# Rings of eight and products four deep in a graph network's row expansions and sums

## What is computed

```python
edge_index = jnp.stack([src, dst])
...
x = _layernorm(x + _L1_gnn_ref(x, edge_index, L1_gnn_W, L1_gnn_b), axis=-1)
x = _layernorm(x + _L2_gnn_ref(x, L2_gnn_weight1, L2_gnn_weight2, src, dst), axis=-1)
x = _layernorm(x + _L3_gnn_ref(x, edge_index, edge_attr_16, batch0, L3_gnn_W, L3_gnn_a), axis=-1)
```

```python
h_src = feat_n[src]
copy_sum = jax.ops.segment_sum(h_src, dst, num_segments=N)
```

## Time and profile before

| | us |
|---|---|
| median of three runs | 16084.6 |
| lowest and highest | 16077.82, 16091.67 |
| the profiled execution | 16079.79 |
| its span | 16078.1 |

### The profile page before, as it was taken

One profiled execution on the slowest core, in us unless ns is written; L12 is line 12 of the kernel. 1 busy time (PEld: TensorE's weight loads), 2 busy tenths in 40 slices (PEclk: granted clock), 3 DMA queues, 4 the chain that ended last, 5 costly groups with the idle time before them and its releaser, 6 DMA issues. The chain is left out here.

```text
span 16078.1 us, 333902 instructions
## 1 busy us (share of the span) xinstructions
PE 10302.2 (64%) x72558; PEld 7980.5 (50%) x72559; DVE 10167.2 (63%) x36116; ACT 4495.2 (28%) x11901; POOL 9058.1 (56%) x10038
## 2 busy tenths in 40 slices
PE   6555555555537777767965656645566776667886
PEld 5333333333326666656853444422344664336886
DVE  9666666666643444437856777752365666887887
ACT  0111111111102333322113430025301223556886
POOL 0477777777745777767764445546400555554442
PEclk9777777777766777765556667755555665557998
DMA  9722222222242444453319997756653897885665
GB/s 369 303 80 79 81 81 79 79 83 79 79 94 58 80 80 80 80 79 71 68 28 279 324 309 223 224 163 218 191 176 89 279 278 257 270 267 204 212 212 160
DMA packets 2144346, 2589.93 MB, mean 161 GB/s; under 512 B 892242, under 2 KB 1761819, under 8 KB 2144195
## 3 DMA queue, kind: packets, MB, share of 16 engines
q1 hardware_dynamic: 1749158, 1741.66, 37.6%
q0 software_dynamic: 353792, 655.17, 13.1%
q10 hardware_dynamic: 41244, 191.56, 3.1%
HBM read 1738.44 MB, written 848.86 MB: 161 GB/s over the span
## 5 line engine op out<-in xcount | busy, mean ns | idle before, releaser
L566 POOL DMA_INDIRECT edges_by_dst<-rec,pos x1568 | 1541.2, 983 | 1029.1 <-DVE rec L501 555.5
L989 POOL DMA_INDIRECT sc_rows<-src_table,sc_idx x1664 | 1589.1, 955 | 607.9 <-issue 497.6
L566 POOL DMA_INDIRECT edges_by_cell<-rec,pos x1568 | 1545.5, 986 | 514.8 <-issue 497.4
L1756 PE MATMUL ex_rows<-table,ex_oh 128*128 x6528 | 1132.6, 339 | 884.8 <-DVE ex_stage L1732 335.7
L1844 PE MATMUL gs_part<-gs_rows,gs_oh 128*128 128x192 bf16 x6528 | 1024.4, 321 | 602.0 <-DVE gs_oh L1817 518.5
L1756 PEld LDWEIGHTS ex_rows<-table,ex_oh 128*128 128x128 bf16 x6528 | 724.9, 129 | 1292.3 <-issue 1252.6
L642 PE MATMUL xps<-ident,ea 128*128 128x128 f32 x784 | 216.4, 431 | 1740.9 <-DMA ea<-in_edge_attr_dram 1740.9
L1844 PEld LDWEIGHTS gs_part<-gs_rows,gs_oh 128*128 128x128 bf16 x6528 | 697.0, 131 | 929.3 <-issue 613.5
L2224 ACT ACTIVATE key_in_block<-at_rows,first_node 128x66 f32<-128x66 f32 x4352 | 1083.3, 336 | 266.2 <-PE at_part L2252 244.9
L2252 PE MATMUL at_part<-cell_edge_term,key_in_block 128*66 128x128 f32 x8704 | 1062.7, 286 | 115.3 <-issue 96.4
L530 DVE SCALAR_TENSOR_TENSOR junk<-rowb,keycol,earlier 128x128 f32<-128x128 f32 (+1 forms) x3136 | 1124.5, 415 | 1.8
(11 more groups left out here) (402 smaller groups left out, 27327.5 us busy)
## 6 DMA issues: line engine op xcount, KB each, us to landing
ex_keys<-src_key_rows SPq DMA_DIRECT2D x1632, 128.0 KB
gs_rows<-dst_rows_by_src SPq DMA_DIRECT2D x1088, 192.0 KB
rowb<-sort_key_rows SPq DMA_DIRECT2D x392, 512.0 KB, 5.2
ex_keys<-dst_key_rows SPq DMA_DIRECT2D x1088, 128.0 KB
dst_rows_by_src<-patY ACTq DMA_DIRECT2D x1, 104448.0 KB, 417.2
rows_by_src<-ex_stage SPq DMA_DIRECT2D x544, 192.0 KB
scored_dst_rows_by_src<-patZ ACTq DMA_DIRECT2D x1, 71808.0 KB, 637.9
scored_rows_by_src<-ex_stage SPq DMA_DIRECT2D x544, 132.0 KB
```

The lines of the kernel that those rows point to most:

```text
L566: nc.gpsimd.indirect_dma_start(out=out, out_offset=bass.IndirectOffsetOnAxis(ap=pos[:, u, k, j:j + 1], axis=0), in_=row, in_offset=None).t ...
L989: nc.gpsimd.indirect_dma_start(out=rows[:, u, j, :], out_offset=None, in_=tabS, in_offset=bass.IndirectOffsetOnAxis(ap=idx[:, u, j:j + 1], ...
L1756: m = nc.tensor.matmul(rows[k][u % 2][r // 2][:, r % 2, 0:W], oh[k][:, u % 2, r * P:(r + 1) * P], t3[:, bass.ds(held[k][u], 1), :].rearran ...
```

## The change

In `expand_rows`, a call with one list (ex2) gets rings of R = 8 key and staging slots and loops of eight steps, and one-hots and PSUM buffers that are four deep; with two lists (ex1) R = 4 and two deep stay. `sum_rows` gets four one-hot buffers and makes them three groups ahead (gs1 and gs2). `attention_rows` gets four one-hot and four PSUM buffers a list and makes the one-hots three ahead in place of two. `skewed` takes the number of steps of a turn as `ring`.

```diff
-def skewed(eng, n, stages, enter=None):
+def skewed(eng, n, stages, enter=None, ring=RING):
...
-        for u in range(RING):
-            step(i, u, 0 if isinstance(i, int) and i == 0 else None, RING if last else None)
+        for u in range(ring):
+            step(i, u, 0 if isinstance(i, int) and i == 0 else None, ring if last else None)
...
-    n = D.NG // RING
     lists = [q for q in ((0, K.krA, toA), (1, K.krB, toB)) if q[2] is not None]
+    R, deep = (RING, 2) if len(lists) == 2 else (2 * RING, 4)
+    n = D.NG // R
...
-        keys = {k: sb(f"keys{k}", [P, RING, SLOTS * P], BF16) for k, _, _ in lists}
-        oh = {k: sb(f"oh{k}", [P, 2, SLOTS * P], BF16) for k, _, _ in lists}
-        stage = {k: sb(f"stage{k}", [P, RING, SLOTS, W], BF16) for k, _, _ in lists}
-        rows = {k: [[ctx.enter_context(nc.psum_tensor(f"{name}_rows{k}{u}{h}", [P, 2, 256], F32)) for h in range(2)] for u in range(2)]
+        keys = {k: sb(f"keys{k}", [P, R, SLOTS * P], BF16) for k, _, _ in lists}
+        oh = {k: sb(f"oh{k}", [P, deep, SLOTS * P], BF16) for k, _, _ in lists}
+        stage = {k: sb(f"stage{k}", [P, R, SLOTS, W], BF16) for k, _, _ in lists}
+        rows = {k: [[ctx.enter_context(nc.psum_tensor(f"{name}_rows{k}{u}{h}", [P, 2, 256], F32)) for h in range(2)] for u in range(deep)]
...
-                        wait(sp, s_oh[k], g - RING + 1)
+                        wait(sp, s_oh[k], g - R + 1)
...
-                        wait(dve, s_mm[k], g - 1)
+                        wait(dve, s_mm[k], g - deep + 1)
...
-                skewed(dve, n, [(2, turn), (0, evict)])
+                skewed(dve, n, [(deep, turn), (0, evict)], ring=R)
...
-                        wait(pe, s_ev[k], g - 1)
+                        wait(pe, s_ev[k], g - deep + 1)
...
-        oh = {k: sb(f"oh{k}", [P, 2, P, SLOTS], BF16) for k, _, _ in lists}
+        oh = {k: sb(f"oh{k}", [P, RING, P, SLOTS], BF16) for k, _, _ in lists}
...
-                        wait(dve, s_mm[k], g - 1)
-                        nc.vector.tensor_tensor(oh[k][:, u % 2, :, :], K.iota4[:, :, :],
+                        wait(dve, s_mm[k], g - RING + 1)
+                        nc.vector.tensor_tensor(oh[k][:, u, :, :], K.iota4[:, :, :],
...
-                skewed(dve, n, [(1, onehots), (0, add)], blocks)
+                skewed(dve, n, [(3, onehots), (0, add)], blocks)
...
-        oh = [sb(f"oh{k}", [P, 2, SLOTS * P], BF16) for k in range(2)]
+        oh = [sb(f"oh{k}", [P, RING, SLOTS * P], BF16) for k in range(2)]
...
-        rows = [[ctx.enter_context(nc.psum_tensor(f"{name}_rows{k}{u}", [P, SLOTS, W], F32)) for u in range(2)] for k in range(2)]
+        rows = [[ctx.enter_context(nc.psum_tensor(f"{name}_rows{k}{u}", [P, SLOTS, W], F32)) for u in range(RING)] for k in range(2)]
...
-                skewed(dve, n, [(2, turn), (0, evict)])
+                skewed(dve, n, [(3, turn), (0, evict)])
...
-                        wait(pe, s_ev[k], g - 1)
+                        wait(pe, s_ev[k], g - RING + 1)
```

More of the change, by code:

```diff
@@ L697, in step @@
                 continue
-            run(i + q // RING, q % RING)
+            run(i + q // ring, q % ring)
     for s in range(-first, 0):
-        step(0, s, 0, n * RING)
+        step(0, s, 0, n * ring)
     def body(i, last):
@@ L704, in body @@
             enter(i)
-        for u in range(RING):
-            step(i, u, 0 if isinstance(i, int) and i == 0 else None, RING if last else None)
+        for u in range(ring):
+            step(i, u, 0 if isinstance(i, int) and i == 0 else None, ring if last else None)
     loop(eng, n, body)
-    for s in range(RING, RING + lastly):
-        step(n - 1, s, None, RING)
+    for s in range(ring, ring + lastly):
+        step(n - 1, s, None, ring)
 class Count:
@@ L1677, in expand_rows @@
         s_ev = {k: counts.get(f"expand_evicted{k}") for k, _, _ in lists}
-        s_out = {k: [counts.get(f"expand_stored{0 if back else k}{u}", back or k == 0) for u in range(RING)] for k, _, _ in lists}
+        s_out = {k: [counts.get(f"expand_stored{0 if back else k}{u}", back or k == 0) for u in range(R)] for k, _, _ in lists}
         with nc.Block() as block:
@@ L1694, in store @@
                                      stage[1][:, u, :, :].rearrange("p r c -> p (r c)")).then_inc(s_out[1][u].sem, 16)
-                skewed(sp, n, [(4, load), (-1, store)])
+                skewed(sp, n, [(4, load), (-1, store)], ring=R)
                 for k, _, _ in lists:
-                    for u in range(RING):
+                    for u in range(R):
                         wait(sp, s_out[k][u], n * 16)
@@ L1741, in evict @@
                         wait(act, s_out[1][u], i * 16)
-                        nc.scalar.copy(stage[1][:, u, 0:2, :], rows[1][u % 2][0][:, :, 0:W])
-                        nc.scalar.copy(stage[1][:, u, 2:4, :], rows[1][u % 2][1][:, :, 0:W]).then_inc(s_ev[1].sem, 1)
-                skewed(act, n, [(0, evict)])
+                        nc.scalar.copy(stage[1][:, u, 0:2, :], rows[1][u % deep][0][:, :, 0:W])
+                        nc.scalar.copy(stage[1][:, u, 2:4, :], rows[1][u % deep][1][:, :, 0:W]).then_inc(s_ev[1].sem, 1)
+                skewed(act, n, [(0, evict)], ring=R)
             @block.tensor
@@ L1761, in blocks @@
                     for k, _, _ in lists:
-                        held[k] = nc.values_load_multi_w_load_instructions(K.cblk[0:1, k, bass.ds(i * RING, RING)], engines=PE_ONLY,
+                        held[k] = nc.values_load_multi_w_load_instructions(K.cblk[0:1, k, bass.ds(i * R, R)], engines=PE_ONLY,
                                                                            min_val=0, max_val=D.blocks - 1, skip_runtime_bounds_check_because=CLAMPED)[1]
-                skewed(pe, n, [(0, products)], blocks)
+                skewed(pe, n, [(0, products)], blocks, ring=R)
         for k, _, _ in lists:
@@ L1843, in products @@
                         for r in range(SLOTS):
-                            m = nc.tensor.matmul(part[k][u][:, 0, :], oh[k][:, u % 2, :, r], rows[k][:, u, r, :],
+                            m = nc.tensor.matmul(part[k][u][:, 0, :], oh[k][:, u, :, r], rows[k][:, u, r, :],
                                                  start=r == 0, stop=r == SLOTS - 1)
@@ L1913, in turn @@
                         wait(dve, s_key[k][u], (i + 1) * 16)
[L1914 to L1915 removed]
+                        wait(dve, s_mm[k], g - RING + 1)
+                        nc.vector.tensor_scalar(oh[k][:, u, :], keys[k][:, u, :], K.iotac[:, :], None, ALU.is_equal).then_inc(s_oh[k].sem, 1)
                 def evict(i, u):
```

32 lines of the change are left out of this document (16 added, 16 removed).

## The result

The changed kernel takes 15,896.9 us (median of four runs, 15,888.2 to 15,899.6) against 16,081.2 us (16,077.2 to 16,091.7) for the kernel before: a ratio of 0.988, 95% interval 0.987 to 0.990. It is 184 us faster, where 272 us were forecast. Its profiled execution has a span of 15,897.9 us, that of before 16,078.1 us.

A forecast was written before the change was run, and what follows sets the result against it. It took staging slots to bound ex2, a DVE-PE ping-pong gs2, DVE's instructions gs1 and SyncE's stream ex3. 16079.8 - 125 (ex2) - 147 (gs2) = 15808, stated as 15810 us, range 15760 to 15905.

The forecast's parts named there:

- the ring of staging slots: ex2: four staging slots are the limit, 5.71 us for four groups; with eight slots the ring serves eight groups.
- POOL at 1.265 us a group: ex2: POOL's scatter issues are the next limit, 688 us plus a 6.25 us head, 694 in all; gain 125 us.
- rivals A: ex2: POOL's issue lengthens beside busy DVE and ACT, 1.44 us a group, 15903 us in all; chance 0.08.
- A2: ex2: full port lock, a one-hot before every issue, 1.61 us a group, 882 us, 15995 in all; chance 0.03.
- ACT's waits for the store: ex2: ACT's waits for a store to land would be gone after the change, as a sign of the forecast.
- The ping-pong: gs2: DVE and PE alternate with one one-hot ahead; removing two waits, 0.59 and 0.55 us, takes 4.48 to 3.34 a turn.
- the load ring: gs2: four slots for loaded rows are late next, 3.51 us a turn; 3.4 was taken, gain 147 us.
- the landing: gs2: time from a load's issue to its product, 2.51 us for the stage's first load, within 3.48 when steady.
- Rival B: gs2: the load ring takes over at 4.8 us a turn, 45 us lost, 16000 us in all; chance 0.06.
- SyncE's 7.64 us a turn: ex3: SyncE's own instruction stream sets the stage at 7.64 us for four groups, untouched by the change; gain 0.
- chance of 0.03 for slower: Whole kernel: chance of measuring slower, from ex3's eviction behind keys three ahead not being covered, 16128 us.
- The high end: Whole kernel: upper bound 15900 us, with gains of 100 and 80, gs2's turn at 3.9 us and POOL at 1.31.

The follow-up runs named there:

- e9: The changed kernel, but layer three's expansion has only the rings of eight, with two one-hots and two product buffers: 15,871.0 us, ratio 0.989.
- e10: The changed kernel, but layer three's expansion has only four one-hots and four product buffers, with rings and loops of four: 16,156.6 us, ratio 1.007.
- e4: The changed kernel with eight slots for loaded rows and loops of eight groups in layer three's sums: 15,767.1 us, ratio 0.982.
- e8: As e4, loops of eight groups in layer three's sums, but the loaded rows keep four slots: 15,890.1 us, ratio 0.990.
- e1: The kernel before with only the change to layer three's expansion: 15,973.6 us, ratio 0.995.
- e2: The kernel before with only the changes to the sums and the attention rows: 16,161.1 us, ratio 1.007.
- e5: The kernel before with 34 satisfied waits on SyncE ahead of the attention rows' loop: 16,086.4 us, ratio 1.002.
- e7: e4 with 24 satisfied waits on SyncE ahead of the attention rows' loop: 15,741.2 us, ratio 0.981.
- e3: The kernel before with 34 no-operations on SyncE ahead of the attention rows, absent from the compiled program: 16,049.2 us, ratio 1.000.
- e6: e2 with 16 satisfied waits on VectorE ahead of the maximum stage's loop: 15,982.7 us, ratio 0.996.

## Why the prediction was right, and where not

**ex2: right, by its own steps; the gain less so.** The limit was the ring of staging slots (e9 and e10 part it cleanly: slots alone 719.6 us, product buffers alone 831.5 us), and POOL at 1.265 us a group was next, as forecast. 697.7 us measured from first load to last scatter, 694 forecast. Of the 129 us gained 6 are behind that, at the stage's end. That 129 lies so near the forecast 125 is in part luck: both are taken from the first profile's stage, and in the experiments, where the old ex2 takes 829 to 835 us and the new 719 to 720, the gain is some 113 us. Why the old ex2 is 13 us apart between the two I do not know. Neither form of contention came (rivals A and A2): the scatter stayed at 0.96 us in the rows above, 967 ns in the mean, with VectorE's one-hots as frequent as forecast. 503 of the 544 scatters ran beside a one-hot and took 968 ns, the other 41 took 959 ns. The shared-port rule of the Trainium skill ("SBUF — State Buffer", SBUF: two separate sides) made a stage of 882 us of it, and this trace doesn't show that lock either. The miss was ACT's waits for the store, which I expected to vanish.

**gs2: the mechanism right, one term mis-sized.** The ping-pong went away and the load ring took over, as the text had it. I took 3.40 us a turn, "between DVE's 3.24 and the ring's 3.51", and it is 3.75. That is 136 x 0.35 = 48 us, nearly all of the 51 that are missing. The failed step is the landing, the time from a load's issue until its product starts. The ring's own term, 1.00 us and a landing of 2.51, was worked out from the stage's first, cold load, and I then went below it to 2.4, because the steady pattern bounded the landing by 3.48 us only from above and I took the cold load for the slowest sort. The changed kernel's trace shows the split: over groups 40 to 519 it is 0.95 us from a product's start to the next issue of its slot and 2.79 us from the issue until the product starts, 3.74 together. In the rows above it is 0.90 and 2.49. Of the 2.79 us 2.22 pass until the load's last packet has ended, and 0.57 more until the product. So a landing at a DMA share of 0.71 was not quicker than the cold one of 2.51 but slower. That the ring is the limit is shown by e4 and e8. Rival B had the right mechanism with an exaggerated price, 4.8 us a turn.

**ex3: wrong, and by no rival.** I wrote that SyncE's 7.64 us a turn were untouched, and listed the instructions of the loop as the whole of its cost. They are untouched; their place is not. The edit to ex2 moved the loop by 34 instructions, and each turn pays 0.26 us since. e1 shows that it comes without ex3's edit, e2 that ex3's edit is free, e5 that 34 idle instructions are enough, e7 that 24 more take it away.
**mx3, and what could have happened.** The changed kernel lost 7 us there, 0.2 us a turn, with another compiled body of VectorE's loop. The cause of that is open: e1 has a body of the same length and took 1,142.5 us. That it wasn't 200 us hung on that body's length and place, which nothing in the edit aims at: the sums' and attention rows' edits alone (e2) come out slower than the kernel before, although gs2 gains 90 us in them. My chance of 0.03 for slower had no case of this kind in it.

**gs1** changed by -4 us of 1,062 at an equal 7.03 us a turn, as forecast.

The sum: 129 + 96 - 39 = 186, and 4 - 7 - 3 for the others, is 180 us between the spans. The total lay within the range, 8 us from its upper end, and that is in part luck. The high end allowed gs2 67 us less of a gain, of which its miss took 51, and POOL's issues 25 us, which they did not need. The 39 us of ex3, which no step had foreseen, happened to fit into what was left.

## What to carry to other kernels

When an edit changes how often a loop is unrolled, every later loop of the same engine moves in its program; look at their turns one by one, and at the packets of the "instruction" queue, before blaming the edit's own mechanism. A loop turn that gets longer with no wait, no longer instruction and the same count is the sign, and a few satisfied waits ahead of the loop are the test (the bare no-operations of e3 did not survive compiling). And where a ring is said to be next, price it by a loaded round trip, at the traffic it will have, and don't take less than the cold one: here it was 2.8 us, not 2.4.

## What the runs showed of the hardware that I had not expected

A loop on VectorE of 272 instructions costs 31.8 or 38.3 us a turn by a shift of a single instruction, 203 us over the stage; one on SyncE of 54 instructions costs 7.64 or 7.90 us. In the first case the "instruction" queue carries 154 more packets, in the second none (114 in e5, 115 before), so a body for which nothing more is fetched still pays a little, at the branch and at one place inside.

The last stage, at3, shows a smaller step of the same kind: e2 and e6 differ by sixteen instructions on VectorE, and it takes 1,430.8 us in the one and 1,452.1 us in the other. It is at 1,449 to 1,452 us in e4, e7 and e8 too, where VectorE's loop lies 54 or more instructions later than in the changed kernel, and at 1,429 to 1,435 us in all the others. What in the body pays for it I did not find; it is some 20 us that e7 leaves.

TensorE's clock followed the load ring: in gs2 it was granted 0.59 in the changed kernel and 0.61 in e8, where PE stops for a load about once in four groups, and 0.99, that is 2.4 GHz, in e4, where it does so three times. The products' busy time fell from 396.8 us for 2,175 matmuls to 274.5 for 2,144. No run parts what this alone brought: with 0.52 us for a group's four products in place of 0.76, slots also come free sooner.
